# A graph-network kernel: the compare that makes gather one-hots writes two bytes an entry, and ScalarE narrows them

## The chip, the cores and the metric

One core of one Trainium2 chip. The metric is the device time of one execution, in microseconds (us). TensorE does the matrix products, VectorE (DVE) and ScalarE (ACT) the elementwise work, GpSimd (POOL) constants and indirect transfers, SyncE (SP) issues the transfers.

## The reference

Four graph layers, one after another, on 12500 nodes with 64 features and 200000 edges (`src`, `dst`, sorted by `dst`). Cut to the parts that matter here:

```python
edge_index = jnp.stack([src, dst])
h = jnp.maximum(_layernorm(x), 0.0)
x = x + L0(h, edge_attr_64, src, dst, ...)     # mean over edges, two batch-normed products
h = jnp.maximum(_layernorm(x), 0.0)
x = x + L1(h, edge_index, edge_attr_8, ...)    # product per edge, sum over edges
h = jnp.maximum(_layernorm(x), 0.0)
x = x + L2(h, src, dst, ...)                   # twice: mean of h[src] over the edges of each dst
h = jnp.maximum(_layernorm(x), 0.0)
x = x + L3(h, edge_index, ...)                 # normalised sum of h[row] over the edges of each col
```

The last two layers need three times the same operation: `segment_sum(h[src], dst)`, a gather of node rows by edge and a sum by destination.

## The kernel before

The first two layers go over the edges with indirect transfers (`edge_pass`). The last two layers use `cell_pass`, three times, which gathers and sums with one-hot matrices on TensorE. These matrices depend only on the edges. `cells_setup` builds them once, between the second and the third layer.

`cells_setup` cuts the edges into 75 cells of 2688 edges (128 partitions x 21 tiles). In each cell it ranks the edges by the page of their source node (98 pages of 128 nodes, 32 slots a page) and writes to DRAM (`cells_d`) for each cell a matrix of 128 x 3136 single bytes (98 pages x 32 slots): entry (p, slot) is 1.0 if the edge in that slot reads node p of the page. That matrix is made like this: TensorE sums per slot the node number within its page, plus 1 (`ps_low`, L1032); ScalarE copies it to `lows` (L1067); SP stores it to `lows_d` as one row of 3136 two-byte numbers (L1081) and loads this row back to all 128 partitions (`low_rows`, L1086); VectorE compares it with the partition's own number plus 1 (`next_id`), result `rows` (L963); SP stores `rows` to `cells_d` (L1090).

The stage is one block in which TensorE, ScalarE, VectorE and SP each run a program of turns, one turn per cell and two more at the end, 4 turns to a pass of the loop (`over_cells`, L751). They are ordered by semaphores: `hold(engine, semaphore, value)` waits and then counts up a tick (L175 and L176 are inside these helpers). In turn r the order within each engine is:

- VectorE: L926 and L930 take the maximum over pages for cell r; L935, L936; L939 and L945 make the slot one-hots of cell r; L952 makes the page one-hots of cell r + 2; L891 to L915 handle edges beyond a page's 32 slots; L963 is the compare for cell r - 2.
- TensorE: L977 and L979 (after L935), then L989, L996, L1001, L1009 for cell r + 1 (L1009 after ScalarE's L1057; L926 of the next turn waits for it), then L1019 and L1023 for cell r - 2, then L1032, L1035, L1038 for cell r - 1.
- ScalarE: L1057 copies the sums of L989 and L979; L1060 and L1061 for cell r - 2; L1067, L1068, L1069 copy the results of L1032 to L1038 for cell r - 1.
- SP: L1081, L1086 for cell r, then L1090 for cell r - 2.

`rows` has four buffers, `low_rows` and `lows` two. The next block (columns and words of the schedule, L1104 to L1138) begins when all stores have landed.

Of the kernel before, what the change touches and what calls it, by code (L numbers as in the profile page):

```python
# [19 lines left out]
BF16 = mybir.dt.bfloat16  # L20
FP8 = mybir.dt.float8e4
# [56 lines left out]
def build(nc, a):  # L78

    ctx = ExitStack()  # L80
    with ctx:
# [679 lines left out]
        def cells_setup():  # L761
# [31 lines left out]
            def room(n):  # L793
                at[0] += n
                return arena[:, at[0] - n:at[0]]
# [13 lines left out]
            lows = [room(CAP // 2).bitcast(BF16)[0:WINDOWS, :] for _ in range(2)]  # L809
            low_rows = [room(WINDOWS * CAP // 2).bitcast(BF16) for _ in range(2)]  # L810
            rows = [room(CELL_ROW) for _ in range(4)]
            cells_b, spots_b, both_b = (room(n).bitcast(BF16) for n in (PAGES // 2, 8, CAP // 2))
            assert at[0] <= ARENA
            ps_rank = ps_all[:, 0:2560].rearrange("p (b n) -> p b n", n=512)
# [11 lines left out]
            with nc.Block() as block:  # L826
# [51 lines left out]
                "cell", "sums", "summed", "prefix", "top", "over", "rank", "rank_hot", "slots"))  # L878
            s_spot, s_spot_int, s_spot_hot, s_mats, s_lows, s_row, s_hot, s_taken, s_spread = (sem(f"s_c_{n}") for n in (
                "spot", "spot_int", "spot_hot", "mats", "lows", "row", "hot", "taken", "spread"))  # L880
            s_lows_out, s_out = sem("s_c_lows_out"), [sem(f"s_c_out{k}") for k in range(4)]
            s_low_rows = [sem(f"s_c_low_rows{k}") for k in range(2)]

            with nc.Block() as block:
                @block.vector
                def _(dve):
# [33 lines left out]
                    def body(it, r):  # L920
                        g0 = it * step
                        if within(it, r, 0, step):
                            here = bass.ds((g0 + r) * CELL_TILES, CELL_TILES)
                            hold(dve, s_prefix, g0 + (r + 1))
                            whole = CELL_TILES // BANK_TILES
                            nc.vector.tensor_reduce(  # L926
                                top[:, 0:whole * BANK_TILES].rearrange("p (b t) -> p b t", b=whole),
                                ps_rank[:, 0:whole, 0:BANK_TILES * PAGES].rearrange(
                                    "p b (t w) -> p b t w", w=PAGES)[:, :, :, 0:WINDOWS], AX.X, ALU.max).then_inc(s_top, 1)
                            nc.vector.tensor_reduce(top[:, whole * BANK_TILES:], rank_tiles(whole * BANK_TILES, CELL_TILES),  # L930
                                                    AX.X, ALU.max).then_inc(s_top, 1)
                            hold(dve, s_top, (g0 + r) * 2 + 2)
                            if within(it, r, -2, step):
                                hold(dve, s_spot_hot, g0 + (r - 1))
                            nc.vector.tensor_scalar(over_cap[r % 2], top, MARK + CAP, None, ALU.is_ge).then_inc(s_over, 1)  # L935
                            nc.vector.tensor_scalar(rank, top, MARK, None, ALU.subtract).then_inc(s_rank, 1)  # L936
                            hold(dve, s_rank, g0 + (r + 1))
                            hold(dve, s_slots, g0 + r)
                            nc.vector.tensor_tensor(  # L939
                                rank_hot, lanes[:, 0:CAP].unsqueeze(1).to_broadcast([P, CELL_TILES, CAP]),  # L940
                                over(rank, CAP), ALU.is_equal).then_inc(s_rank_hot, 1)
                            hold(dve, s_rank_hot, g0 + (r + 1))
                            if within(it, r, -2, step):
                                hold(dve, s_mats, g0 + (r - 1))
                            nc.vector.tensor_tensor(  # L945
                                slots[r % 2], rank_hot.unsqueeze(2).to_broadcast([P, CELL_TILES, 3, CAP]),
                                values[:, here, 0:3].unsqueeze(3).to_broadcast([P, CELL_TILES, 3, CAP]),
                                ALU.mult).then_inc(s_slots, 1)
                        if within(it, r, 2, step):
                            if within(it, r, -2, step):  # L950
                                hold(dve, s_mats, g0 + (r - 1))
                            nc.vector.tensor_tensor(  # L952
                                cell_of[(r + 2) % 4], lanes[:, 0:PAGES].unsqueeze(1).to_broadcast([P, CELL_TILES, PAGES]),
                                over(page[:, bass.ds((g0 + (r + 2)) * CELL_TILES, CELL_TILES)], PAGES),
                                ALU.is_equal).then_inc(s_cell, 1)
                        if within(it, r, 0, step):
                            spill_slots(it, r)
                        if within(it, r, -2, step):
                            k = (r - 2) % 4
                            if within(it, r, -6, step):  # L960
                                hold(dve, s_out[k], (it + (r - 2) // 4) * 16)
                            hold(dve, s_low_rows[r % 2], it * (16 * step // 2) + ((r - 2) // 2 + 1) * 16)
                            nc.vector.tensor_scalar(rows[k].bitcast(FP8), low_rows[r % 2], next_id[:, :], None,  # L963
                                                    ALU.is_equal, saturate=False).then_inc(s_hot, 1)

                    over_cells(dve, body, 2, 2, step)

# [77 lines left out]
                @block.scalar  # L1045
                def _(act):
                    def body(it, r):
                        g0 = it * step
                        if within(it, r, 0, step) or within(it, r, 1, step):
                            hold(act, s_sums, g0 + (r + 2))  # L1050
                            lo = 0 if within(it, r, 1, step) else at_over
                            hi = at_over + CELL_TILES if within(it, r, 0, step) else at_over
                            if within(it, r, -1, step):
                                hold(act, s_prefix, g0 + r)
                            if within(it, r, -2, step):
                                hold(act, s_spot, (g0 + r) * 4 - 4)
                            nc.scalar.copy(sums[(r + 1) % 2][:, lo:hi], ps_sums[:, lo:hi]).then_inc(s_summed, 1)  # L1057
                        if within(it, r, -2, step):
                            hold(act, s_spread, g0 + (r - 1))
                            nc.scalar.copy(slot_dst[:, bass.ds((g0 + (r - 2)) * SLOTS_OF, SLOT_TILES)], ps_slot[:, 0:SLOT_TILES])  # L1060
                            nc.scalar.copy(spilled[:, bass.ds((g0 + (r - 2)) * 4, 4)],  # L1061
                                           ps_slot[:, SLOT_TILES:SLOT_TILES + 4]).then_inc(s_row, 1)
                        if within(it, r, -1, step):
                            hold(act, s_mats, g0 + r)
                            if within(it, r, -3, step):
                                hold(act, s_lows_out, (g0 + r) * 16 - 32)
                            nc.scalar.copy(lows[(r - 1) % 2], ps_low).then_inc(s_lows, 1)  # L1067
                            nc.scalar.copy(cells_b[0:2 * CAP, :], ps_cells)  # L1068
                            nc.scalar.copy(spots_b[0:CAP, :], ps_spots).then_inc(s_taken, 1)  # L1069

                    over_cells(act, body, 1, 2, step)

                @block.sync
                def _(sp):
                    sp.dma_start(past_d[1:2, :, :].rearrange("o p e -> p (o e)"), scratch_f).then_inc(s_target, 16)

                    def body(it, r):
                        g0 = it * step
                        if within(it, r, 0, step):
                            hold(sp, s_lows, g0 + (r + 1))  # L1080
                            sp.dma_start(lows_d[bass.ds(g0 + r, 1), :].rearrange("o (w r) -> w (o r)", r=CAP),  # L1081
                                         lows[r % 2]).then_inc(s_lows_out, 16)
                            hold(sp, s_lows_out, (g0 + (r + 1)) * 16)
                            if within(it, r, -2, step):
                                hold(sp, s_hot, g0 + (r - 1))
                            sp.dma_start(low_rows[r % 2], lows_d[bass.ds(g0 + r, 1), :].to_broadcast(  # L1086
                                [P, WINDOWS * CAP])).then_inc(s_low_rows[r % 2], 16)
                        if within(it, r, -2, step):
                            hold(sp, s_hot, g0 + (r - 1))
                            sp.dma_start(cells_d[bass.ds(g0 + (r - 2), 1), :, :].rearrange("o p n -> p (o n)"),  # L1090
                                         rows[(r - 2) % 4]).then_inc(s_out[(r - 2) % 4], 16)
# [929 lines left out]
```

## Time and profile before

| | us |
|---|---|
| median of 3 runs | 8393.72 |
| lowest and highest | 8385.75, 8405.17 |
| profiled execution, whole | 8393.79 |
| profiled execution, span of its instructions | 8392.1 |

The span runs from the first to the last instruction; 1.7 us of the profiled execution lie around it. A row of busy time adds up an engine's instructions; it can hide a stage where another engine sets the pace, so it is read by stretch of time.

### The profile page before, as it was taken

How to read it: one execution, taken by the hardware profiler on the slowest of the kernel's cores; microseconds unless marked ns; L12 is line 12 of the kernel's file. 1: busy time of each engine (PE TensorE's matmuls, PEld its weight loads, DVE VectorE, ACT ScalarE, POOL GpSimd, SP SyncE). 2: the span in 40 equal slices, each digit the busy share in tenths (PEclk: the TensorE clock that was granted, in tenths of full speed). 3: DMA queues.
4: the chain of work that ended last, by engine and by line, in shares of the span. 5: the costliest groups of instructions: out<-in, count | busy, mean ns of one | idle time of the engine just before them, and what ended most of it. 6: DMA issues, size and time to landing. Idle time of an engine off the chain costs nothing. (4 is left out here: it accounts for less than half of the span.)

```text
span 8392.1 us, 233180 instructions
## 1 busy us (share of the span) xinstructions
PE 4773.5 (57%) x79177; PEld 3915.3 (47%) x79178; DVE 4437.4 (53%) x12947; ACT 2019.8 (24%) x3234; POOL 3358.8 (40%) x3400
## 2 busy tenths in 40 slices
PE   1222222222444445444545777858877689977897
PEld 1222222222244444444444666645555556664665
DVE  4334343344655544455447888866777413551255
ACT  1111111111311111111110000025433355425543
POOL 5777777777077777777770000001000010001000
PEclk7556655555766666666666788769998799978999
DMA  2222222222033323333221322336543366526654
GB/s 86 59 58 61 59 60 58 58 59 53 17 95 90 90 88 89 90 90 89 88 75 48 92 87 87 91 132 227 197 144 132 124 234 214 188 83 243 227 199 163
DMA packets 310092, 928.23 MB, mean 111 GB/s; under 512 B 85284, under 2 KB 110500, under 8 KB 278425
## 3 DMA queue, kind: packets, MB, share of 16 engines
q1 hardware_dynamic: 175524, 794.74, 27.9%
q0 software_dynamic: 107552, 114.03, 6.1%
q10 hardware_dynamic: 26656, 16.06, 0.6%
q14 instruction: 306, 2.51, 0.1%
q8 instruction: 54, 0.88, 0.0%
HBM read 724.40 MB, written 200.13 MB: 110 GB/s over the span
## 5 line engine op out<-in xcount | busy, mean ns | idle before, releaser
L556 POOL DMA_INDIRECT store<-table,store x3136 | 3137.5, 1000 | 1038.4 <-issue 955.1
L709 PE MATMUL ps_all<-store 128*128 128x65 bf16 (+1 forms) x18816 | 996.3, 233 | 1704.3 <-DVE store L628 1545.2
L709 PEld LDWEIGHTS ps_all<-store 128*128 128x128 bf16 x18816 | 949.0, 124 | 1755.8 <-issue 1755.8
L1227 PE MATMUL ps_all<-store 128*128 128x192 bf16 x13416 | 1482.0, 253 | 208.8 <-issue 82.3
L1297 ACT CAST store<-ps_all 128x768 bf16<-128x768 f32 x1350 | 1076.5, 798 | 1277.1 <-PE ps_all L1379 1206.2
L1227 PEld LDWEIGHTS ps_all<-store 128*128 128x128 bf16 x13416 | 1073.4, 99 | 522.8 <-issue 499.2
L1255 POOL DMA_INDIRECT store<-table_b,spill_row x225 | 213.5, 949 | 2134.6 <-PE ps_all L1379 1973.0
L731 PE MATMUL ps_all<-wide,store 128*128 x9408 | 511.5, 236 | 807.4 <-DVE store L644 807.4
L1323 DVE TENSOR_SCALAR store<-lanes,turned 128x256 bf16<-128x256 bf16 x4446 | 887.0, 281 | 26.9 <-DVE turned L1319 22.5
L731 PEld LDWEIGHTS ps_all<-wide,store 128*128 128x128 bf16 x9408 | 480.9, 127 | 832.9 <-issue 832.5
L628 DVE TENSOR_SCALAR store<-lanes,place_of 128x256 bf16<-128x256 bf16 x3136 | 690.4, 303 | 62.9 <-DVE place_of L624 62.0
L684 DVE TENSOR_TENSOR store<-store 128x512 f32<-128x512 f32 x196 | 135.7, 692 | 1096.6 <-DMA store<-table,store 1096.6
L1234 DVE TENSOR_REDUCE turned<-ps_all 128x64 f32<-128x192 f32 x516 | 183.2, 355 | 926.1 <-PE ps_all L1227 887.5
L422 POOL MEMSET wide<- 128x384 bf16 x4 | 1.7, 418 | 1433.5 <-POOLq L1101 1082.2
L594 ACT CAST store<-store 128x512 bf16<-128x512 f32 x392 | 244.4, 623 | 1124.9 <-DVE store L656 1100.7
L1379 PE MATMUL ps_all<-wide,store 128*32 128x192 bf16 x11172 | 402.0, 259 | 119.6 <-issue 64.8
L681 DVE TENSOR_TENSOR store<-ps_all,store 128x512 f32<-128x512 f32 x196 | 135.0, 689 | 632.9 <-DMA store<-table,store 626.2
L1379 PE MATMUL ps_all<-wide,turned 128*32 128x192 bf16 x10878 | 397.8, 263 | 92.5 <-issue 73.8
L603 ACT CAST store<-store 128x512 bf16<-128x512 f32 x196 | 122.9, 627 | 1158.1 <-DVE store L684 1158.1
L600 ACT ACTIVATE store<-store 128x512 bf16<-128x512 f32 x196 | 125.3, 639 | 1066.2 <-DVE store L681 1066.2
L1379 PEld LDWEIGHTS ps_all<-wide,store 128*32 128x32 fp8e4 x11172 | 223.1, 99 | 261.8 <-issue 261.4
L1379 PEld LDWEIGHTS ps_all<-wide,turned 128*32 128x32 fp8e4 x10878 | 221.1, 100 | 232.9 <-issue 232.6
(235 smaller groups left out, 5417.1 us busy)
## 6 DMA issues: line engine op xcount, KB each, us to landing
store<-pairs_d SPq DMA_DIRECT2D x150, 1664.0 KB, 7.0
pairs_d<-store SPq DMA_DIRECT2D x75, 1664.0 KB, 6.2
store<-in_dst_rows SPq DMA_DIRECT2D x196, 512.0 KB
store<-lows_d SPq DMA_DIRECT2D x75, 784.0 KB, 4.9
store<-in_edge_attr SPq DMA_DIRECT2D x196, 256.0 KB, 2.7
store<-table,store POOLq DMA_INDIRECT x3136, 2.4
store<-cells_d SPq DMA_DIRECT2D x114, 392.0 KB, 3.7
turned<-cells_d SPq DMA_DIRECT2D x111, 392.0 KB
```

The source lines that it names most:

```text
L556: nc.gpsimd.indirect_dma_start(rows_f[:, g % SLOTS, j, :], None, table, bass.IndirectOffsetOnAxis(ap=src[:, g * TILES + j:g * TILES + j + ...
L594: nc.scalar.copy(value[slot][:, :, 1, 0:D], rows_f[:, slot, :, :]).then_inc(s_mid, 1)
L628: last = nc.vector.tensor_scalar(onehots[:, k, j, :], lanes[:, :], place[:, j:j + 1], None, ALU.is_equal)
L684: nc.vector.tensor_tensor(v, side[:, slot, 0:TILES * D], v, ALU.add).then_inc(s_begun, 1)
L709: last = nc.tensor.matmul(ps_pair[r % 2][:, b * width:(b + 1) * width], onehot[r % 2][b][:, j, :], value[r][:, j, i, 0:width], start=(b == ...
L731: last = nc.tensor.matmul(ps_hid[:, r % 2, j * D:(j + 1) * D], onehot_t[b][:, j, :], split[:, bass.ds(w + b, 1), i, :].rearrange("p o d -> ...
L1227: last = nc.tensor.matmul(to, pairs_hot[k][:, q, half * P:(half + 1) * P], rows[:, q, :] if q < SLOT_TILES else spill, start=(q == 0), sto ...
L1234: return nc.vector.tensor_reduce(sums[k], of.rearrange("p (i d) -> p d i", i=PARTS), AX.X, ALU.add)
L1255: nc.gpsimd.indirect_dma_start(spill[:, g, :], None, table_b, bass.IndirectOffsetOnAxis(ap=spill_row[:, g:g + 1], axis=0)).then_inc(s_fetc ...
L1297: nc.scalar.copy(picked[r % 2][:, c * PICK:(c + 1) * PICK, :], of).then_inc(s_evicted, 1)
L1323: last = nc.vector.tensor_scalar(pairs_hot[k][:, q, :], lanes[:, :], place[k][:, q:q + 1], None, ALU.is_equal)
L1379: last = nc.tensor.matmul(ps_pick[(r + 1 + c) % 2][j * CAP:(j + 1) * CAP, q, 0:PARTS * D], gather_hot[k][:, w * CAP:(w + 1) * CAP], split[ ...
```

## The change

VectorE's compare writes its result as two-byte numbers to one new buffer, `rows_wide`. ScalarE gets a copy at the end of its turn that reads `rows_wide` and writes the single bytes to `rows`. VectorE waits for ScalarE's previous copy before it writes `rows_wide` again. The wait for an old store of `rows` moves from VectorE to ScalarE. SP's load of the next `low_rows` waits for the compare (new semaphore `s_wide_hot`), its store of `rows` for ScalarE's copy (`s_hot`).

```diff
@@ cells_setup @@
             rows = [room(CELL_ROW) for _ in range(4)]
+            rows_wide = room(2 * CELL_ROW).bitcast(BF16)
...
+            s_wide_hot = sem("s_c_wide_hot")
...
@@ VectorE @@
                         if within(it, r, -2, step):
-                            k = (r - 2) % 4
-                            if within(it, r, -6, step):
-                                hold(dve, s_out[k], (it + (r - 2) // 4) * 16)
+                            if within(it, r, -3, step):
+                                hold(dve, s_hot, g0 + (r - 2))
                             hold(dve, s_low_rows[r % 2], it * (16 * step // 2) + ((r - 2) // 2 + 1) * 16)
-                            nc.vector.tensor_scalar(rows[k].bitcast(FP8), low_rows[r % 2], next_id[:, :], None,
-                                                    ALU.is_equal, saturate=False).then_inc(s_hot, 1)
+                            nc.vector.tensor_scalar(rows_wide, low_rows[r % 2], next_id[:, :], None,
+                                                    ALU.is_equal).then_inc(s_wide_hot, 1)
@@ ScalarE, after L1069 @@
+                        if within(it, r, -2, step):
+                            k = (r - 2) % 4
+                            hold(act, s_wide_hot, g0 + (r - 1))
+                            if within(it, r, -6, step):
+                                hold(act, s_out[k], (it + (r - 2) // 4) * 16)
+                            nc.scalar.copy(rows[k].bitcast(FP8), rows_wide, saturate=False).then_inc(s_hot, 1)
@@ SP, before the load L1086 @@
                             if within(it, r, -2, step):
-                                hold(sp, s_hot, g0 + (r - 1))
+                                hold(sp, s_wide_hot, g0 + (r - 1))
                             sp.dma_start(low_rows[r % 2], lows_d[bass.ds(g0 + r, 1), :].to_broadcast(
                                 [P, WINDOWS * CAP])).then_inc(s_low_rows[r % 2], 16)
```

## Rows read from the trace of the kernel before

**Rows 1.** The page, part 1: busy us of each engine, share of the span, instructions

```profile
PE 4773.5 (57%) x79177; PEld 3915.3 (47%) x79178; DVE 4437.4 (53%) x12947; ACT 2019.8 (24%) x3234; POOL 3358.8 (40%) x3400
```

**Rows 2.** All instructions of L963: duration in ns (min/median/max), first and last start

```profile
L963 DVE TENSOR_SCALAR store<-store,next_id x75: 1844/1847/1855, 4541.2 to 5535.2; 128x3136 fp8e4<-128x3136 bf16 x75
```

**Rows 3.** Busy time by stretch: us and (count) of each engine, granted clock, DMA

```profile
4541.20:5535.20 994.00, 762.98 (x11508) 649.29 (x11506) 873.49 (x1225) 84.64 (x442) 0.00 (x0) 0.79 0.30 90
...
5500.00:5540.00 40.00, 23.43 (x383) 20.67 (x381) 25.06 (x35) 3.12 (x22) 0.00 (x0) 0.63 0.44 142
```

**Rows 4.** Waits, 4541.2 to 5535.2: who waited for whom, total us, times, longest

```profile
PE ps_all L977 <- DVE store L935: 221.9, 72, 4.0
...
DVE store L945 <- DVE store L939: 25.4, 72, 0.4
```

**Rows 5.** Timeline of one cell: start, duration, instruction, [idle before <-releaser]

```profile
5003.90 1.58 PE L1009 MATMUL ps_all<-store,turned 128*128 128x490 bf16 x10
...
5007.32 1.85 DVE L963 TENSOR_SCALAR store<-store,next_id 128x3136 fp8e4<-128x3136 bf16 x1
...
5008.96 0.16 ACT L1069 CAST store<-ps_all 32x16 bf16<-32x16 f32 x1
5009.09 2.19 DVE L926 TENSOR_REDUCE store<-ps_all 128x20 f32<-128x1960 f32 x1
...
5012.19 0.18 PE L977 MATMUL ps_all<-store,turned 128*128 128x21 bf16 x1 [3.73 <-DVE store L935]
...
5015.01 0.51 ACT L1057 CAST store<-ps_all 128x421 bf16<-128x421 f32 x1 [5.89 <-PE ps_all L989]
...
5017.57 1.58 PE L1009 MATMUL ps_all<-store,turned 128*128 128x490 bf16 x10
...
5021.11 1.85 DVE L963 TENSOR_SCALAR store<-store,next_id 128x3136 fp8e4<-128x3136 bf16 x1
```

**Rows 6.** Timeline of the last cells of the stage

```profile
5499.73 1.84 DVE L963 TENSOR_SCALAR store<-store,next_id 128x3136 fp8e4<-128x3136 bf16 x1
...
5504.59 0.18 PE L977 MATMUL ps_all<-store,turned 128*128 128x21 bf16 x1 [2.42 <-DVE store L935]
...
5511.01 1.85 DVE L963 TENSOR_SCALAR store<-store,next_id 128x3136 fp8e4<-128x3136 bf16 x1
...
5516.02 0.17 PE L977 MATMUL ps_all<-store,turned 128*128 128x21 bf16 x1 [0.27 <-DVE store L935]
...
5522.42 1.85 DVE L963 TENSOR_SCALAR store<-store,next_id 128x3136 fp8e4<-128x3136 bf16 x1
...
5528.59 1.85 DVE L963 TENSOR_SCALAR store<-store,next_id 128x3136 fp8e4<-128x3136 bf16 x1 [4.33 <-DMA store<-lows_d]
...
5535.22 1.85 DVE L963 TENSOR_SCALAR store<-store,next_id 128x3136 fp8e4<-128x3136 bf16 x1 [4.78 <-DMA store<-lows_d]
5540.06 0.33 SPq L1138 DMA_DIRECT2D past_d<-wide  x1
```

**Rows 7.** Groups of VectorE's instructions, whole span: count, busy us, mean ns, idle before

```profile
L1323 DVE TENSOR_SCALAR store<-lanes,turned 128x256 bf16<-128x256 bf16 x4446 | 887.0, 281 | 26.9 <-DVE turned L1319 22.5
...
L644 DVE TENSOR_SCALAR store<-store,node_id 128x1024 bf16<-128x1024 int32 x392 | 276.6, 746 | 36.3 <-issue 31.5 <-DMA wide<-attr_d 4.7
...
L963 DVE TENSOR_SCALAR store<-store,next_id 128x3136 fp8e4<-128x3136 bf16 x75 | 138.6, 1848 | 9.1 <-DMA store<-lows_d 9.1
...
L1319 DVE TENSOR_SCALAR turned<-wide,first 128x26 f32 (+1 forms) x171 | 41.2, 241 | 200.0 <-issue 200.0
...
L935 DVE TENSOR_SCALAR store<-store 128x21 bf16<-128x21 f32 x75 | 13.8, 184 | 20.5 <-DVE store L930 20.2
```

**Rows 8.** Groups of ScalarE's instructions, whole span

```profile
L416 ACT CAST wide<-agg 128x3136 bf16<-128x3136 f32 x8 | 22.4, 2805 | 5.6 <-DVE agg L392 5.6
```

**Rows 9.** Queue instructions of VectorE at one back edge of the loop

```profile
L751 DVEq COMPARE_BRANCH  x1: 80/80/80, 4609.7 to 4609.7; - x1
...
L175 DVEq FUSED_REGOPS  x1: 53/53/53, 4610.3 to 4610.3; - x1
```

## The prediction

> **What bounds the kernel now.** I read the page first [rows 1]: no engine is busy for more than 57% of the span, so the whole-kernel shares decide nothing and the stage of the change has to be read alone. The 75 executions of the changed compare (L963) start between 4541.2 and 5535.2 us [rows 2]; that is the stage, 994 us of 8392. The view of busy time by stretch [rows 3] shows what kind of stage it is: VectorE is busy 873 of its 994 us, TensorE 763, ScalarE only 85, GpSimd nothing. Then the view of waits over the same stretch [rows 4]: TensorE waits 221.9 us for VectorE's L935 (72 times, about 3 us in each cell), while VectorE's own waits are for its own previous result (L945 for L939, 25.4 us in all; L935 and L939 have two more rows of this pattern, 19.9 and 18.6 us). Nobody makes VectorE wait in the steady state; its queue, in program order, sets the period. So a microsecond taken out of VectorE's cell is a microsecond off the period until TensorE's slack is used up.
>
> The timeline of one cell [rows 5] says the same in order: L926 comes straight behind L963, its start even overlapping the end by 0.08 us (L963 starts at 5007.32 and takes 1.85, L926 starts at 5009.09, 1.77 later). The next L963 starts at 5021.11. The period is 13.79 here; from first to last over the first 71 starts it is (5499.73 - 4541.20) / 70 = 13.69 us [rows 5, 6].
>
> **The change, part by part.**
>
> *The compare.* Before, VectorE reads 3136 two-byte entries and writes 3136 one-byte entries in 1848 ns [rows 7]. After, it writes two-byte entries to one buffer, rows_wide. No row shows this compare at 3136 with a two-byte output, but the same form (a compare of two-byte entries with a per-partition number, two-byte result) stands at 256 entries: 281 ns (L1323) [rows 7]. Its rate has to be found. L644 and L963 are also compares with a per-partition number, one from four-byte input, one to one-byte output. Between them: (1848 - 746) / (3136 - 1024) = 0.522 ns an entry, with a fixed part of 1848 - 3136 x 0.522 = 212 ns. If the two-byte form has the same fixed part, its rate is (281 - 212) / 256 = 0.27 ns, that is half of 0.522. I take exactly half: 212 + 3136 x 0.261 = 1030 ns. (The same at 256 entries gives 279 ns, where 281 is measured.) The saving is 1848 - 1030 = 0.82 us a cell.
>
> Bounds: the only unsure part is the fixed one. If it is as large as a small compare-like instruction with a per-partition operand takes (L1319, 26 entries, 241 ns), the rate is 40 / 230 = 0.174 ns and the compare takes 281 + 2880 x 0.174 = 0.78 us. If it is as small as L935 (21 entries, two-byte result, 184 ns), the rate is 97 / 235 = 0.413 and the compare takes 1.47 us [rows 7]. Savings 1.07 and 0.38 us. I stay at 1.03, because L963 and L644 are of the form nearest to it.
>
> The Trainium skill, "VectorE: DVE Perf Modes", section "The perf-mode tier table", gives four results a cycle to a one-source operation with two-byte input and output, 693 ns at 2048 entries; an estimate from it, at the 0.96 GHz that the page gives, is 693 + 1088 / 4 / 0.96 = 976 ns at 3136, and the sum below would come out 4 us lower by it.
>
> *The copy on ScalarE.* New: 75 copies of 3136 two-byte entries to one-byte entries, in ScalarE's program after L1067 to L1069 of the same turn. No row has ScalarE writing one-byte entries. The nearest has the same count: 128x3136 from four-byte to two-byte takes 2805 ns (L416) and the rate is the same from PSUM (L1057: 421 entries in 0.51 us; (2805 - 510) / 2715 = 0.845 ns) [rows 5, 8]. I take 2.80 us. A lower end is not to be had, since ScalarE's rate does not change with input type or memory in these rows; as the upper end I take twice this, 5.6 us, because on VectorE the one-byte output costs twice the rate of the two-byte output.
>
> Where it lies [rows 5]: L1069 ends at 5009.12, the new compare would end at 5008.35, so the copy runs from 5009.2 to 5012.0. Queued behind it on ScalarE is L1057 of the next turn, which now starts at 5015.01 and would start 0.82 earlier, 5014.2, after 2.2 us of idleness. Even a late L1057 hurts only when TensorE's L1009 waits for it; L1009 starts at 5017.57, shifted 5016.75, and L1057 takes 0.51. So the copy may take 7.0 us before it costs anything in the steady state. Both ends of my bound are under it: the cost is zero there.
>
> *The waits.* VectorE's wait for the store of four cells ago moves to ScalarE; in its place VectorE waits for ScalarE's previous copy, which ended some 8 us earlier (5012.0 against the next compare at 5020.3). On SP's queue the load L1086 now waits for the compare instead of the bytes, and that compare is a turn's work back. The store L1090 waits for ScalarE's copy; in the same turn of SP's program, L1081 before it already waits for ScalarE's L1067 of one turn later, which stands behind that copy in ScalarE's order, so L1090 adds no wait. No DMA is added or enlarged, and the two-byte buffer never goes to DRAM. At the back edge of the loop (16 times) VectorE's sequencer takes its branch at 4609.7, beside the compare's start (4609.8), and its queue events for the next instruction end by 4610.4: a compare of 1.03 us still covers them [rows 9].
>
> *TensorE.* It idles 3.73 us before L977 in the cell shown and 2.42 in the last loaded one, where the granted clock of the stretch is 0.63 [rows 3, 5, 6]. After: 2.9 and 1.6. It stays covered. Cost nothing; if the cover went, the rest of the gain would go with it.
>
> *The end of the stage* [rows 6]. The last two compares wait for a DMA (5528.59 and 5535.22), and the last one's bytes must be stored before the next block starts at 5540.06. This end gets longer: the last compare is 0.82 shorter, but 2.80 of copy and about 0.06 of handing over follow it: +2.04 us. Of the others, 71 have their full saving in front of a loaded VectorE. The compare at 5511.01 is met by TensorE, which was idle only 0.27 us before L977 at 5516.02: it gives 0.27. The compare at 5522.42 is followed by a wait for DMA and gives nothing.
>
> *Sum:* 71 x 0.82 = 58.2, plus 0.27, minus 2.04 = 56.4 us. The blocks before and after are separate and follow each other, so it reaches the end of the program. The profiled execution took 8393.79 us (span 8392.1 and 1.7 around it), the median of the runs is 8393.72: **8337.4 us**, 0.67% less. With the two bounds of the compare: 71 x 1.07 + 0.27 - 1.79 = 74.4, giving 8319; 71 x 0.38 + 0.27 - 2.48 = 24.8, giving 8369. The upper bound of the copy adds 2.8.
>
> **The rivals.**
> - *A: the compare does not get faster.* If the input side or the per-partition number sets VectorE's rate, the two-byte result also takes 1.85 us. Nothing is saved, the end of the stage still has the copy: 8393.8 + 2.86 = 8396.7, no measurable change. Against it: 281 ns at 256 entries would need a fixed part of 147 ns, and L963 and L644 show 212 [rows 7]. Chance 0.06.
> - *B: ScalarE becomes the bound, and the kernel is slower.* The loop would be: L1057 (0.51, with its hand-over 0.7), then TensorE from L1009 to L1038 and ScalarE to the end of L1069 (5003.90 to 5009.12, 5.2), then the copy, then L1057 again. The period is 5.9 us plus the copy [rows 5]. It decides from 7.0 us of copy on, and the kernel is slower than before from 7.8. At three times L416, 8.4 us, the period is 14.3, 0.6 over the present one: +44 us over 73 cells and 7.6 at the end, 8445 us. For it: no row has ScalarE writing single bytes. Against it: its rate is the same 0.845 ns between rows of 421 and 3136 entries, from PSUM and from SBUF [rows 5, 8]. Chance 0.03. The Trainium skill, "ScalarE: Activation LUTs", section "Rules for kernel authors", advises VectorE over ScalarE for simple elementwise work; here that would speak against the copy, and the trace agrees on the rates (2.80 us against about 1) but shows ScalarE idle nine tenths of the stage.
> - *C: the two-byte compare lands at the slow bound*, 1.47 us: 8369. Chance 0.05.
>
> **How the numbers follow.** The forecast, 8337.4, has 0.86; its own range, with a hundred nanoseconds on the compare and a few microseconds of run-to-run scatter, is 8326 to 8349. The range for 8 in 10 takes in the bounds of the compare: 8319 to 8369. What a measurement of this kernel can tell from no change is about 0.2%, 17 us (the three runs shown are 19 us apart). Faster: forecast and C, 0.90. Within: A, 0.07. Slower: B, 0.03.
>
> **What would show it.** In the changed profile: 75 compares of 128x3136 with a two-byte result at about 1.03 us; 75 copies on ScalarE at about 2.80 us, 210 us more busy time there; compare to compare 12.87 us on average instead of 13.69; L926 still directly behind the compare; L1057 still waiting for TensorE and not for ScalarE; TensorE's wait for L935 down from 3.1 to 2.3 us a cell; first to last compare 994 down to about 936 us; after the last compare 2.9 us of copy before the last store. It would be wrong if L926, L891 or L945 got a wait on another engine, if the copy took more than 7 us, or if a stage outside this one moved by more than a few microseconds.

## The result, and the profile after

The changed kernel took 8318.61 us (median of 4 runs, 8309.45 to 8326.78) against 8396.99 (4 runs, 8385.75 to 8405.17): ratio 0.9907, interval 0.989 to 0.9924, 78 us less. The prediction was 8337.4 with a range of 8319 to 8369: the direction is right, the time lies 19 us below the forecast and 0.4 us outside the range. Two later comparisons of the same pair gave ratios 0.9936 and 0.9931; they are told below, and so is a third, from a set of runs in which the kernel before itself took 10011 us.

First the changed compare and the new copy, in the groups of instructions by line (these answer to the L963 row of [rows 7] and to [rows 8]).

```profile
L964 DVE TENSOR_SCALAR store<-store,next_id 128x3136 bf16<-128x3136 bf16 x75 | 77.3, 1030 | 10.2 <-DMA store<-lows_d 10.2
```

```profile
L1076 ACT CAST store<-store 128x3136 fp8e4<-128x3136 bf16 x75 | 210.2, 2803 | 7.6 <-DVE store L964 7.6
```

1030 ns and 2803 ns: the two prices that no row of before showed are what was worked out, 1.03 and 2.80 us. (The compare is now L964; VectorE's lines in this stage are 2 higher, TensorE's and ScalarE's 1 higher, SP's 7 higher.)

All instructions of the compare (answers to [rows 2]), and the stage in busy time by stretch (answers to the first row of [rows 3]).

```profile
L964 DVE TENSOR_SCALAR store<-store,next_id x75: 1027/1030/1037, 4552.4 to 5484.9; 128x3136 bf16<-128x3136 bf16 x75
```

```profile
4552.40:5484.90 932.50, 757.65 (x11510) 643.17 (x11508) 813.03 (x1226) 286.48 (x516) 0.00 (x0) 0.80 0.33 96
```

From the first compare to the last it is 932.4 us where it was 994.0. VectorE lost 60 us of work, ScalarE gained 202 and is still idle for two thirds of the stage. The waits of that stretch (answers to [rows 4]) show that no new one has come in front of VectorE, and that TensorE's wait for it went from 221.9 to 166.3 us, which is 0.77 us a cell.

```profile
ACT wide L1061 <- PE ps_all L1024: 342.0, 71, 5.5
...
PE ps_all L978 <- DVE store L937: 166.3, 72, 3.1
ACT store L1058 <- PE ps_all L990: 113.6, 71, 2.5
DVE store L947 <- DVE store L941: 25.3, 72, 0.4
```

The timeline of one cell (answers to [rows 5]):

```profile
5002.37 1.03 DVE L964 TENSOR_SCALAR store<-store,next_id 128x3136 bf16<-128x3136 bf16 x1
5003.31 2.19 DVE L928 TENSOR_REDUCE store<-ps_all 128x20 f32<-128x1960 f32 x1
5005.29 0.16 ACT L1070 CAST store<-ps_all 32x16 bf16<-32x16 f32 x1
5005.35 2.80 ACT L1076 CAST store<-store 128x3136 fp8e4<-128x3136 bf16 x1
...
5009.17 0.51 ACT L1058 CAST store<-ps_all 128x421 bf16<-128x421 f32 x1 [1.02 <-PE ps_all L990]
...
5015.20 1.03 DVE L964 TENSOR_SCALAR store<-store,next_id 128x3136 bf16<-128x3136 bf16 x1
```

L928 (L926 before) starts straight behind the compare, 0.94 us after its start instead of 1.77. The copy runs at once after ScalarE's last small copy, and L1058 behind it still waits for TensorE, 1.02 us here. The end of the stage (answers to [rows 6]):

```profile
5479.19 1.04 DVE L964 TENSOR_SCALAR store<-store,next_id 128x3136 bf16<-128x3136 bf16 x1 [5.54 <-DMA store<-lows_d]
...
5480.43 2.80 ACT L1076 CAST store<-store 128x3136 fp8e4<-128x3136 bf16 x1 [2.62 <-DVE store L964]
...
5484.87 1.04 DVE L964 TENSOR_SCALAR store<-store,next_id 128x3136 bf16<-128x3136 bf16 x1 [4.65 <-DMA store<-lows_d]
5486.41 2.81 ACT L1076 CAST store<-store 128x3136 fp8e4<-128x3136 bf16 x1 [3.03 <-DVE store L964]
5492.18 0.33 SPq L1145 DMA_DIRECT2D past_d<-wide  x1
```

From the last compare's start to the next block it is 7.3 us, where it was 4.8. The copy starts 0.20 us after the end of the compare for the last cell but one (5480.23 to 5480.43), and 0.50 us after it for the last (5485.91 to 5486.41).

**Where the profiled execution's 67 us are.** It took 8326.78 us against 8393.79. Aligned instruction by instruction on VectorE, the difference is made of: +11.2 us ahead of the stage (the first compare starts at 4552.4, not 4541.2), -61.6 from the first to the last compare, +2.5 at the end of the stage, -12.4 from there to VectorE's first sum of the next pass over the cells, -9.8 in the first part of that pass, +3.0 in the rest. So the stage itself gives -59.1. The rest comes from stretches that the change does not touch, and two of them are large. Here is the node stage behind the stage, first before, then after, in busy time by stretch; the number behind the five engines' busy times is the granted clock. What this text calls the node stage runs from VectorE's first addition in it to the first sum of the next pass, so the first products of that pass are among the 425.

```profile
5587.20:5638.00 50.80, 39.94 (x425) 32.70 (x424) 26.65 (x68) 14.35 (x19) 7.65 (x8) 0.54 0.25 82
```

```profile
5537.80:5577.80 40.00, 27.78 (x425) 21.21 (x422) 26.66 (x68) 14.37 (x19) 7.64 (x8) 0.79 0.37 132
```

The same 425 products took 39.9 us of TensorE before and 27.8 after, at a mean granted clock of 0.54 and 0.79 (0.50 is the level of 1.2 GHz, 1.00 that of 2.4). The question for the experiments was whether that belongs to the change.

### The profile page after: what moved, and what is told of

Its sections match the earlier page's. It is cut to its first block and busy times, and to the rows that moved or that the text cites. A ratio compares the mean times of both kernels' runs of the same rounds, so it can differ in the third digit from the quotient of the medians.

```text
span 8325.1 us, 233420 instructions
## 1 busy us (share of the span) xinstructions
PE 4736.1 (57%) x79177; PEld 3888.7 (47%) x79178; DVE 4375.2 (53%) x12947; ACT 2226.2 (27%) x3309; POOL 3374.6 (41%) x3400
```

## The experiments

Theory 1: the gain is the compare's shorter time in VectorE's queue, everything else is hidden, and the faster node stage is chance. Theory 2: the change also brings the clock up behind the stage. Two more rivals: the gain comes from the moved waits; ScalarE's copy is nearly on the path.

**a_again: the changed kernel once more**, no edit.

> The changed kernel once more, for a closer ratio and a second profile. The first comparison gave 0.9907 (78 us), while the two profiles show 61.6 us less between the first and the last compare, about 2 us back at the end of the stage, and 17 us in the block behind it, where the granted clock was 0.90 in place of 0.50. Theory 1 (the stage alone): the 17 us are chance of the clock grant; the compares again span 932 us and the ratio is nearer 0.993 (59 us). Theory 2 (the change also brings the clock up behind the stage): the ratio stays at 0.991 and the products behind the stage again run at a granted clock of about 0.9.

Measured: 8335.32 us against 8385.01, ratio 0.9936 (0.992 to 0.9951). First to last compare 933.4 us. The node stage behind the stage:

```profile
5538.00:5589.40 51.40, 39.97 (x425) 32.71 (x423) 26.74 (x69) 14.35 (x19) 7.59 (x8) 0.55 0.26 88
```

51.4 us at 0.55: the changed kernel has the slow node stage too. 50 us are gained without it. Theory 2 falls as a rule for every run.

**narrow_stage: the rate undone, all else kept.** The compare writes single bytes to the staging buffer, ScalarE copies bytes to bytes.

```diff
-            rows_wide = room(2 * CELL_ROW).bitcast(BF16)
+            rows_wide = room(CELL_ROW).bitcast(FP8)
...
-                                                    ALU.is_equal).then_inc(s_wide_hot, 1)
+                                                    ALU.is_equal, saturate=False).then_inc(s_wide_hot, 1)
```

> The changed kernel with one part undone: VectorE's compare writes single bytes to the staging buffer, ScalarE copies bytes to bytes. Theory 1: the compare takes 1.85 us again, the copy is hidden, first to last compare 994 us, the end of the stage 2.9 us longer than before, total 3 us above the kernel before, which is not to be told from it. Rival (the gain comes from the new order of waits or from taking the store wait off VectorE): the stage is still shorter than 980 us with the slow compare. Theory 2 of the clock says nothing here unless a copy on ScalarE raises the clock: then the total is 15 us or more below the kernel before.

Measured: 8390.95 against 8385.01, ratio 1.0008 (0.9997 to 1.0018). The compare and the copy:

```profile
L964 DVE TENSOR_SCALAR store<-store,next_id x75: 1844/1846/1853, 4554.1 to 5545.1; 128x3136 fp8e4<-128x3136 bf16 x75
```

```profile
L1076 ACT COPY store<-store 128x3136 fp8e4<-128x3136 fp8e4 x75 | 210.2, 2803 | 8.7 <-DVE store L964 8.7
```

With the compare at 1.85 us again the whole gain is gone. The moved waits and the second step alone are worth nothing that the time can show. Two small things can be read from the trace. The end of the stage is 3.3 us longer. And the compares span 990.9 us, 3.1 less than before, the period is 13.66 in place of 13.69: the new set of waits is worth 0.03 us a cell. The place can be named. In one turn of four VectorE of the kernel before starts L895 0.43 us after L891, in the others 0.33:

```profile
5004.20 0.18 DVE L891 SCALAR_TENSOR_TENSOR store<-store 128x21 f32<-128x21 bf16 x1
5004.53 0.18 DVE L895 TENSOR_SCALAR store<-store 128x21 int32<-128x21 f32 x1
...
5017.89 0.17 DVE L891 SCALAR_TENSOR_TENSOR store<-store 128x21 f32<-128x21 bf16 x1
5018.32 0.18 DVE L895 TENSOR_SCALAR store<-store 128x21 int32<-128x21 f32 x1 [0.26 <-DVE store L891]
```

Over the first 70 cells this adds up to 2.0 us in both traces of the kernel before, and to nothing in narrow_stage and in the changed kernel. What in the old waits causes it is not shown: VectorE has two waits in front of the compare in either form, one of them for another semaphore.

ScalarE copies 3136 entries in 2803 ns whether they come in as one byte or two.

**copy_twice: ScalarE's copy doubled.**

```diff
+                            nc.scalar.copy(rows[k].bitcast(FP8), rows_wide, saturate=False).then_inc(s_copied, 1)
+                            hold(act, s_copied, g0 + (r - 1))
                             nc.scalar.copy(rows[k].bitcast(FP8), rows_wide, saturate=False).then_inc(s_hot, 1)
```

> The changed kernel with ScalarE's copy done twice, one after the other, 5.6 us in each cell. Theory 1 (up to 7.0 us of copy are free): first to last compare stays at 932 to 936 us, the end of the stage 2.9 us longer, total about 3 us above the changed kernel. Rival (the copy is nearly on the path already): each cell grows by up to 2.8 us, the compares span up to 1140 us.

Measured: 8348.13 against 8385.01, ratio 0.9944 (0.9922 to 0.9966); the compares span 937.4 us, their period over the first 71 starts is 12.845, that of the changed kernel. The 5 us more are in the last few cells, which puts the span 1.4 above the expected 932 to 936, and 2.6 more are at the end of the stage. The median lies 13 us above a_again's, where 3 were expected; the trace shows 8 of them, and the intervals of the two ratios overlap. The timeline:

```profile
5000.45 2.81 ACT L1077 CAST store<-store 128x3136 fp8e4<-128x3136 bf16 x1
5003.37 2.81 ACT L1079 CAST store<-store 128x3136 fp8e4<-128x3136 bf16 x1
5006.08 0.51 ACT L1059 CAST store<-ps_all 128x421 bf16<-128x421 f32 x1
...
5008.52 1.58 PE L1011 MATMUL ps_all<-store,turned 128*128 128x490 bf16 x10
```

ScalarE no longer waits before L1059, so the copy of the sums is late, but TensorE's L1011 needs it only 1.9 us later. The second copy is free in the steady state.

**copy_thrice: the copy tripled**, in the same way, 8.5 us.

> The changed kernel with ScalarE's copy done three times, 8.5 us with the waits between them. By the loop of rival B (0.7 for the copy of the sums, 5.2 from TensorE's prefix products to ScalarE's last small copy, then the big copy) the period becomes 5.9 + 8.5 = 14.4 us, first to last compare about 1045 us, total 8445 to 8455 us, slower than the kernel before by 0.6%. If the cover is larger than I worked out, the period is below 13.7 us and the kernel is not slower than before.

Measured: 8460.62 against 8385.01, ratio 1.009 (1.0073 to 1.0107), 6 us above the expected range. The compares span 1053.0 us, 8 more than expected; the period is 14.35.

```profile
5003.39 0.51 ACT L1059 CAST store<-ps_all 128x421 bf16<-128x421 f32 x1
5004.04 0.18 DVE L894 SCALAR_TENSOR_TENSOR store<-store 128x21 f32<-128x21 bf16 x1 [1.36 <-ACT store L1059]
5004.04 1.58 PE L1011 MATMUL ps_all<-store,turned 128*128 128x490 bf16 x10 [0.80 <-ACT store L1059]
...
5009.26 2.81 ACT L1077 CAST store<-store 128x3136 fp8e4<-128x3136 bf16 x1
5012.18 2.81 ACT L1079 CAST store<-store 128x3136 fp8e4<-128x3136 bf16 x1
5015.10 2.81 ACT L1081 CAST store<-store 128x3136 fp8e4<-128x3136 bf16 x1
5017.82 0.51 ACT L1059 CAST store<-ps_all 128x421 bf16<-128x421 f32 x1
```

This is rival B, made real: L1059 starts with no wait of ScalarE, and both VectorE (L894) and TensorE (L1011) now wait for it. One turn of the loop is 14.43 us here (5003.39 to 5017.82), 14.4 was worked out. So the free room for the copy is between 5.6 and 8.5 us, and the loop that bounds it is the one named.

**b_again: the kernel before against itself**, no edit, in one set of runs with a_third and two others. In this set every run was slower in the passes over the edges ahead of the stage (the first compare starts at 6097.1 us, not 4541.2); the stage itself was the same. Why is open. A different chip is not shown as the cause: the runs carry the same chip number, 15, as those of the set of a_again, whose kernel before took 8385 us.

> The kernel before, once more, against itself. It gives a second profile of it and shows what two sets of runs of one kernel differ by. If the products behind the stage take 51 us at a granted clock of 0.50 or 40 us at 0.76 by chance, this kernel can show either; if the level hangs on the change, it shows 51 us, as its first profile did. The ratio should be 1.000 within 0.002, and the compares span 994 us.

Measured: 10020.69 against 10011.23, ratio 1.0004 (0.9993 to 1.0015). The compares span 995.1 us. The node stage behind the stage:

```profile
7143.30:7184.70 41.40, 27.74 (x424) 21.23 (x422) 26.67 (x69) 14.45 (x19) 7.61 (x8) 0.79 0.37 128
```

The kernel before has the fast node stage as well. That settles the question of Theory 2: both kernels show both levels.

**a_third: the changed kernel in that set.**

> The changed kernel, a third profile and a third set of runs. By theory 1 the ratio lies between 0.992 and 0.995, the compares span 932 to 934 us, and the products behind the stage take 40 or 51 us, either. By theory 2 the ratio is 0.991 and the products take 40 us.

Measured: 9951.4 against 10011.23, ratio 0.9947 (0.9926 to 0.9967), 60 us; compares 932.6 us, node stage behind the stage 53.7 us at 0.54. The same microseconds are gained from a longer program.

**wait_back: VectorE waits for the old store too.**

```diff
+                            if within(it, r, -6, step):
+                                hold(dve, s_out[(r - 2) % 4], (it + (r - 2) // 4) * 16)
                             if within(it, r, -3, step):
                                 hold(dve, s_hot, g0 + (r - 2))
```

> The changed kernel, in which VectorE waits for the store of four cells ago as well, as before the change. The period fell from 13.69 to 12.85 us, 0.03 more than the compare got shorter. If that is the queue work of the wait that was taken away, the period here is 12.87 to 12.88 us, with gaps of 0.43 us before VectorE's third-last small operations in one turn of four; if not, it stays at 12.845.

Measured: period 12.92 us, compares 938.6 us, in a single execution of 9980.32 us in the slower set of runs. The extra 0.07 us a cell is more than the 0.03 expected, and it lies elsewhere: L893 and L897, the L891 and L895 of before, stay 0.32 us apart, and the compare comes late in two turns of four.

```profile
6581.32 0.51 DVE L917 TENSOR_TENSOR store<-store,agg 128x336 bf16<-128x336 bf16 x1
6581.75 1.03 DVE L966 TENSOR_SCALAR store<-store,next_id 128x3136 bf16<-128x3136 bf16 x1
6594.25 0.51 DVE L917 TENSOR_TENSOR store<-store,agg 128x336 bf16<-128x336 bf16 x1
6594.86 1.03 DVE L966 TENSOR_SCALAR store<-store,next_id 128x3136 bf16<-128x3136 bf16 x1
```

From L917 to the compare it is 0.43 us in one turn and 0.61 in the next (0.52 in another, 0.43 in the fourth). The store had been issued four turns, 51 us, earlier, and such stores land within 7 us in the kernel before, so it cannot be what is waited for. The reading that is left, argued and not shown, is the queue's own work for three waits, which the 0.51 us of L917 do not cover; it costs up to 0.18 us in a turn. This kernel has one wait more than before, so it is not the exact undoing of the swap; for the 0.03 us of the swap itself narrow_stage stands. One execution is enough for the period, which agrees within 0.002 us between the other traces of one kernel, but not for a total time.

**busy_pe: can the node stage's clock be had on purpose?** The changed kernel, with 180 products on TensorE (results unused) in the block before that node stage, 90 at its start and 90 after VectorE's first subtraction of parts.

```diff
+                @block.tensor
+                def _(pe):
+                    if begun and keep_busy:
+                        for part in range(2):
+                            if part:
+                                pe.wait_ge(s_dve, dve0 + n_norm + 1)
+                            for _ in range(90):
+                                nc.tensor.matmul(ps_all[:, 0:2 * P], lanes[:, 0:P], lanes[:, :], start=True, stop=True)
```

> The changed kernel with 180 products of 128x256 added on TensorE, results unused, in the block behind the stage, where TensorE idles for 47 us before the products of the node stage. If the granted clock of those products follows what TensorE did before them, they run at a high level each time, take about 40 us in place of 51, and the total falls by up to 11 us against the changed kernel, plus what the first cells of the next pass gain: 8320 to 8330 us, ratio about 0.992. If the grant has nothing to do with it, the block and the node stage stay as they are and the total is that of the changed kernel.

Measured: 9945.34 against 10011.23, ratio 0.9933 (0.9918 to 0.9948); node stage 42.1 us. Only 6 us below a_third, inside the intervals.

**busy_again: the same once more**, in a set in which the kernel before took 8390.38 us, beside **a_fourth**, the changed kernel.

> The run in which TensorE has 180 extra products in the block behind the stage, once more. If TensorE's work before the node stage sets its granted clock, the node stage behind the stage again takes 40 to 42 us at 0.76 or more; if the 42 us of the first such run were chance, 51 us are as likely.

> The changed kernel again, on the chip of the two runs beside it. The compares span 932 to 934 us. The products behind the stage have been seen both ways with it and with the kernel before (40 to 41 us at a granted clock of 0.75, 51 to 54 us at 0.50); either is expected. Ratio to the kernel before 0.993 to 0.995.

Measured: a_fourth 8330.95 against 8390.38, ratio 0.9931 (0.9919 to 0.9943), compares 933.0 us, node stage 50.5 us. busy_again 8321.23, ratio 0.991 (0.9895 to 0.9924), node stage:

```profile
5541.80:5580.40 38.60, 26.28 (x425) 20.47 (x422) 26.68 (x68) 14.38 (x19) 7.71 (x8) 0.82 0.36 122
```

38.6 us. In both traces with the added products this stage is fast, as in the next one; without them it was fast in 3 of 10 traces of this study (before once of two, changed once of four, copy_thrice once; narrow_stage, copy_twice and wait_back not).

**busy_three: the same in three places.** Added products in front of three node stages: 181, 85 and 110.

> The changed kernel with extra products, results unused, in three blocks in which TensorE idles ahead of a node stage: behind the stage of the change (181), ahead of the node stage of the second sum over edges (85) and ahead of that of the fourth layer (110). In the five traces of the changed code looked at, the transposes of the latter two stages spread over 25 to 28 us at a granted clock of 0.50 to 0.63, where the same shape took 17 us at 0.59 to 0.96. If the grant follows TensorE's work before them, each gains 8 to 10 us: ratio to the kernel before about 0.990, 15 to 25 us below the changed kernel. If not, or if the extra products delay the blocks, nothing or a few us of loss.

Measured: 8316.43 against 8390.38, ratio 0.9909 (0.9895 to 0.9924), 14.5 us below a_fourth on the same chip. It is the lowest median of the study, though by ratio the first comparison of the changed kernel (0.9907) is not above it. The node stage behind the stage took 39.0 us. The stretch of the transposes of the second of the three places, first in a_fourth, then here:

```profile
6559.00:6586.60 27.60, 27.60 (x191) 25.03 (x191) 9.13 (x11) 5.47 (x7) 0.00 (x0) 0.50 0.23 99
```

```profile
6555.30:6572.40 17.10, 16.48 (x191) 14.83 (x191) 8.85 (x11) 5.44 (x6) 0.00 (x0) 0.91 0.38 159
```

10.5 us gained there, and none of the 12 traces without added products at this place has it: all show 27.6 us at 0.50. The stage ahead of the second place was slower in this trace (27.6 us of transposes where the other had 19.5), which takes most of it back in this one execution. It is slow so in wait_back and busy_pe as well, where nothing was added near it. In the third place 2.4 us seem gained (28.0 to 25.6), but copy_twice, copy_thrice, b_again and a_third show 25.3 to 25.7 us there without added products, so that says nothing. The difference to busy_again, 5 us, is inside the intervals. That the added products raise the grant of the stage behind them rests on these 3 of 3 traces against 3 of 10, on the second place, and on the times: all eight executions of busy_again and busy_three (8302.5 to 8324.0) lie below all six of a_fourth (8325.2 to 8350.2). That three places are better than one is not shown.

## Why the prediction was wrong, point by point

**The bound.** Right. VectorE's queue sets the period, and 0.82 us out of it came off the period in full: narrow_stage puts the 0.82 back, its period is 13.66 in place of 12.845, and the gain is gone.

**The compare.** Right to the nanosecond: 1030. Half the rate of the byte-writing form with the same fixed part was the right pick between 0.78 and 1.47: from 256 entries in 281 ns to 3136 in 1030 is 0.26 ns an entry. The Trainium skill, "VectorE: DVE Perf Modes", section "The perf-mode tier table", gives four results a cycle for this form, which is by estimate 0.26 ns an entry at the 0.96 GHz of that page, and the trace agrees. The 976 ns that the prediction worked out from it is 54 ns below the measured 1030.

**The copy.** Right: 2803 ns where 2805 was taken, free in the steady state, and the limit of 7.0 us is bracketed by copy_twice and copy_thrice. Per entry ScalarE takes 2.7 times as long as VectorE (2803 against 1030 ns); the "about 1" us that rival B says the trace agrees on was still a forecast for VectorE. Rival B's loop was right in form and size, 14.4 us.

**The waits.** None became a new block. That "VectorE's wait for the store of four cells ago moves to ScalarE" was costed at nothing; with it 0.03 us a cell went away, 2 us in all, at L895.

**The end of the stage.** The hand-over from VectorE to ScalarE was taken as 0.06 us; for the last copy it is 0.50, and with it the end grew by 2.5 us, not 2.04. As a price of a hand-over the 0.50 does not stand: for the two cells before the last ScalarE is idle too, and the copy follows the compare by 0.2 us, and in copy_twice and copy_thrice the last one does as well. What the other 0.30 us are is open.

**The sum** of these for the stage was -56.4 and measures -59.1 (-61.6 and +2.5). Of the 3 us between, 2 are the swapped wait, the rest lies in the last four intervals. (The chances by outcome, 0.90, 0.07 and 0.03, do not quite add up from their parts, which give 0.91, 0.06 and 0.03; nothing hangs on it.)

**The step that failed** is the last: "a few microseconds of run-to-run scatter" in the own range and no term for it in the wider one, together with "a stage outside this one moved by more than a few microseconds" as something that would speak against the mechanism. Stages that the change does not touch move by more than that from execution to execution. The first compare starts at 4541.2 to 4560.8 us over the nine traces of the faster sets, 20 us apart though the code ahead of it is the same, and 5 us apart (4550.0 to 4554.6) among the three of the changed kernel. The node stage behind the stage moves by 11 us between those three. The pass behind it took 253.4 us to the same instruction before and 243.6 after, and 243.6 to 250.2 among the three. In the profiled pair the start made +11.2 us, the node stage and the pass together -22. The prediction had the number for such a term at hand: it says itself that the three runs shown are 19 us apart. Instead the lower end of its range, 8319, was the price of a compare of 0.78 us, which is not what happened: that the time came within 0.4 us of it is chance. In the three comparisons the changed kernel's medians were 8318.6, 8335.3 and 8331.0, and those of before 8397.0, 8385.0 and 8390.4: differences of 78, 50 and 59 us for one and the same change. Two of the three times lie within 7 us of 8337.4. The first lies low; in its profiled run 12 us are the favourable clock grant shown above. The 10 of the pass behind it go with a granted clock that is higher in stretches of it (0.91 against 0.84 from 20 to 60 us, 1.00 against 0.88 from 120 to 140), which is not a proof. Why all four of its runs were low is open: only one of them has a trace.

## What to carry to other kernels

Where one engine's queue sets the period, look at the output type of its widest elementwise operation: the two-byte result halved the time per entry, and an idle engine can do the narrowing even if it needs three times as long as was saved, as long as its turn stays inside the loop that would bound it; work out that loop first. Before setting a range, compare the length of untouched stages between executions: that scatter, here 10 us for a single stage, belongs in the range even where every term of the sum is sure. Waits that never block may still cost something on the engine that sets the period: here 0.03 us a cell went away with one set of them, and 0.07 came with another; that it is the waits themselves is argued, not shown.

## What the runs showed of the hardware that was not expected

TensorE's granted clock in the products of a stage can lie at either level in two executions of the same kernel: the stage took 50.8 and 41.4 us with the kernel before, 40.0 and 51.4 with the changed one. TensorE was nearly idle for the 40 us ahead. The stretch ahead of the node stage, first in the changed kernel (4.3 us busy of 41, clock 0.52), then with added products (26.0 us busy, clock 0.74):

```profile
5496.00:5537.00 41.00, 4.30 (x36) 4.10 (x38) 32.60 (x22) 19.05 (x10) 0.42 (x1) 0.52 0.41 175
```

```profile
5496.00:5537.00 41.00, 25.97 (x194) 21.16 (x194) 33.21 (x23) 17.24 (x8) 0.42 (x1) 0.74 0.36 151
```

Useless products there gave the higher level in 3 of 3 traces, against 3 of 10 without them. The lower level can hold through steady work: in a_fourth TensorE is busy for all of the 27.6 us of the stretch shown above, at 0.50. From the end of a compare on VectorE to the copy on an idle ScalarE it took 0.2 us for the two cells before the last and 0.5 for the last. And one set of runs took 10011 us for a program that took 8385 to 8397 in the others: between the two traces of the kernel before, 1556 us of the difference lie ahead of this stage and 45 behind it, with the stage itself the same within about 1 us.
